# An expert layer's routing in 16 bits, its list and table steps interleaved on VectorE, and a reordered opening of the next layer

## The chip, the cores and the metric

The kernel runs on one core of one Trainium2 chip. The metric is the device time of one execution in microseconds (us). TensorE is called PE here, VectorE DVE, ScalarE ACT, GpSimd POOL; SyncE (SP) issues most of the DMA transfers.

## What is computed

The input x has 4 batches of 512 rows with 288 channels; a condition vector per batch gives shifts, scales and gates. Three transformer layers follow one another, each with 16-head attention. The first one's feed-forward part is a mixture of experts (2 of 4, 1152 hidden channels each), the two others have one dense part. The last stage rotates the rows in the plane of 64 orthonormal columns.

```python
def _L0_cond_ref(x, c, w_adaln, b_adaln, w_qkv, b_qkv, w_proj, b_proj, w_gate, w1, b1, w2, b2):
    ...
    x = x + g_msa[:, None, :] * o
    xn = _modulate(_ln(x), sh_mlp, sc_mlp)
    xf = xn.reshape(-1, C)
    gate_logits = xf @ w_gate
    topk_logits, topk_idx = jax.lax.top_k(gate_logits, TOP_K)
    gates = jax.nn.softmax(topk_logits, axis=-1)
    ...
    hmid = jax.nn.gelu(jnp.einsum('tc,ech->eth', xf, w1) + b1[:, None, :], approximate=True)
    eo = jnp.einsum('eth,ehc->etc', hmid, w2) + b2[:, None, :]
    moe = jnp.einsum('te,etc->tc', cw, eo).reshape(B, N, C)
    return x + g_mlp[:, None, :] * moe
...
U, _ = jnp.linalg.qr(P)
R = _rotation(cond, W, b)
z = jnp.einsum('btn,nd->btd', x, U)
z_rot = jnp.einsum('btd,bde->bte', z, R)
x_rot = x + jnp.einsum('btd,nd->btn', z_rot - z, U)
```

## The kernel before

**Orders.** No scheduler is at work. The order of the instructions on each engine is written out by hand, and semaphores stand between the engines. Each engine takes its queue strictly in order, so a wait on one instruction holds all that stand behind it. A product in 32 bits is made of three passes over operands split into a high and a low part: ACT rounds the high part, DVE subtracts to get the low part, and PE multiplies high by high, high by low and low by high. DVE's dependent small steps are joined by `link` (a semaphore that DVE raises and then waits for itself).

**Routing in layer one.** For each batch b, DVE computes from the gate logits which two of the four experts a row chooses (`gate_ranks(b)`, the tile `rank` of zeros and ones, and `rank_totals`). PE multiplies `rank` by a strictly triangular matrix and by ones (`ranks(b)`, L2033 to L2039), which gives every row its number within its expert; `slots(b)` on DVE turns them into slot numbers, `slot_hits(b)` compares these with a ramp, and `tokens(b)` on PE (L2073, L2077) finds the rows of the first tile with them. `keep_clock(bank, n)` on PE issues n dummy products (L2045).

**Tiles.** The 2048 rows, each chosen twice, are gathered in 11 tiles of up to 512 rows of one expert. A unit j is (tile t, chunk m) = divmod(j, 9): the hidden chunk `tile_hidden(j)` (L1636, 7 matmuls of 512 columns), gelu and high part on ACT, the low part `tile_parts(j)` on DVE (L2992), and two units later `tile_second(j - 2)` on PE (L2114, 12 matmuls of 288 columns). Which rows go in which tile is known late: `first_tokens` casts the list of tile 0 (L2802), POOL gathers its rows with four indirect transfers, and PE turns them (`turn_first`, L2064), with ACT and DVE making high and low part (`first_low`, L2970 and L2973). `tile_places` and `tile_table` (L2878 to L2937) are some 45 small DVE steps that work out the place and the expert of every tile. For the lists of tiles 1 to 10, `list_hits(b)` (L2825 eight times, L2827 once) makes one-hot rows and columns of batch b, `list_products(b)` on PE (L2052) multiplies them, and `token_lists` casts the sum (L2832). SP waits for that cast, loads each list as an index (L769), and POOL gathers the rows of tile 1. `turn_tile(1, c)` (L2089) turns them, one chunk c of three after each of units 6, 7 and 8.

**Weights.** `split_lo_first(0, kind, i)` are low parts of tile 0's weights (kind "1" for the first product, "2" for the second, three pieces each: L3130 with the tail L3131, and L3127); the later tiles' pieces are split at fixed units (`tile_pieces`). SP's loads stand in a fixed order: a big weight of the last stage (L828) after the landing of tile 1's rows, and tile 2's weights behind it.

**Afterwards.** `gate_weights` computes the two mixing weights of each row and `row_places` the place of each row's two results in the stored output (L2939 to L2950). In layer two's opening, POOL gathers the results by them, ACT weighs them (`weigh(k, b)`, L1433), DVE adds them to the residual (`combine_pair(b)`), normalises batch b (`moments`, `rsqrt`, `normalise`, ends in L2498), PE turns the normalised rows (L1699) at the places that `TURN_AT[1]` names, ACT modulates them (`turned`, L1423 and L1427), DVE makes the low part (`low`), and PE multiplies by the weights of queries, keys and values. In `TURN_AT`, the key (b, m) means: after the m-th product of batch b (0 to 4 queries and keys, 5 to 8 values); the value (b', chunks) names what is turned there. A finished chunk leaves PE's bank by ACT (`qk_hi`) and DVE (`qk_rest`, L2535).

## Time and profile before

| | us |
|---|---|
| median of three runs (1562.21 to 1564.72) | 1562.62 |
| the profiled execution | 1557.15 |
| its span | 1555.4 |
| PE busy in it | 1444.6 (93%) |
| DVE busy | 1220.6 (78%) |
| ACT busy | 931.0 (60%) |
| POOL busy | 724.0 (47%) |

The span is the time from the first to the last recorded instruction of the profiled execution; the time around it is 1.75 us. Busy shares are means over the whole span, and PE leads over most of it: what counts for the time is where PE stands still. A row of a timeline gives start, length, engine, line, operation, what is written and read, the shape, the count of records, and in brackets the idle time before it with what ended it. The length of one row may overlap the next, so steps are best read from start to start.

### The profile page before, as it was taken

To read this page: it belongs to the slowest core of one execution; us is meant where nothing else is said; L and a number is where in the kernel's file an instruction comes from. 1 tells how busy PE (TensorE), PEld (TensorE's weight loads), DVE (VectorE), ACT (ScalarE), POOL (GpSimd) and SP (SyncE) were. 2 spreads that over 40 slices of the span, in tenths; PEclk is the share of its full clock that TensorE was granted. 3 is DMA by queue.
4 is the path that set the end of the run, shared out by engine and by line. 5 is a ranking of instruction groups with operands and counts; after the bars stand their busy time and mean duration, and the time that the engine had idled before them with its cause. 6 is when DMAs were issued, how large, how long until landed. Compare 5 with 4: busy or idle time off the path is not lost.

```text
span 1555.4 us, 26822 instructions
## 1 busy us (share of the span) xinstructions
PE 1444.6 (93%) x8987; PEld 986.7 (63%) x8987; DVE 1220.6 (78%) x2469; ACT 931.0 (60%) x1687; POOL 724.0 (47%) x1620
## 2 busy tenths in 40 slices
PE   6899999996999999996999998888999999899998
PEld 5653334875999988885633345877865333378885
DVE  7789996886898687668889987677967999866643
ACT  4458887543666654565478886434734888754432
POOL 0555650114566533036556667676766666650000
PEclk9999999988999999997999999999998999999999
DMA  7765530127555654336735423101165453100001
GB/s 209 227 172 125 144 82 2 38 86 228 160 154 131 184 136 125 93 121 200 237 84 153 115 38 47 6 5 21 18 204 164 119 141 91 6 3 1 1 1 61
DMA packets 108245, 160.70 MB, mean 103 GB/s; under 512 B 33860, under 2 KB 75830, under 8 KB 107976
## 3 DMA queue, kind: packets, MB, share of 16 engines
q1 hardware_dynamic: 101964, 142.85, 30.2%
q0 software_dynamic: 6144, 16.14, 8.5%
q8 instruction: 72, 1.18, 0.3%
q14 instruction: 65, 0.53, 0.1%
HBM read 114.74 MB, written 39.58 MB: 99 GB/s over the span
## 4 chain that ended last, share of the span: by engine, by line
PE 72%; DVE 18%; issue 3%; ACT 3%; DMA 2%; POOL 1%; SPq 1%; DVEq 0%; ACTq 0%; POOLq 0%
PE psum L1636 22%; PE psum L1826 12%; PE psum L1815 9%; PE psum L1789 9%; PE psum L2114 7%; PE psum L2252 5%; DVE bn L2462 1%; PE psum L1699 1%; PE psum L1965 1%; DVE hid_lo L3146 1%; POOL moe_y_end L1179 1%; DVE x_norm L2490 1%; PE psum L2392 1%; PE psum L2089 1%; DVE minus_max L2650 1%
## 5 line engine op out<-in xcount | busy, mean ns | idle before, releaser
L1555 ACT ACTIVATE probs<-psum 128x512 f32<-128x512 f32 x768 | 401.9, 601 | 85.9 <-PE psum L1815 85.3
L2650 DVE TENSOR_REDUCE minus_max<-psum 128x1 fp32r<-128x512 f32 x450 | 288.3, 682 | 36.5 <-PE psum L1789 35.1
L1636 PE MATMUL psum<-x_split,w_hi 128*128 128x512 f32 (+1 forms) x684 | 246.4, 403 | 17.0 <-issue 6.1
L1789 PE MATMUL psum<-k_stack,q_stack 54*128 54x512 f32 x768 | 245.5, 455 | 11.6 <-DMA k_stack<-qk_parts_d 3.3
L1815 PE MATMUL psum<-q_stack,k_stack 55*128 55x512 f32 x768 | 243.2, 450 | 0.6 <-ACT probs L1555 0.6
L1082 POOL TENSOR_TENSOR qr_m<-qr_m 64x8 f32<-64x8 f32 (+35 forms) x544 | 198.4, 365 | 42.6
L1826 PE MATMUL psum<-probs,o_t 128*19 128x512 f32 x1536 | 206.4, 610 | 6.1 <-ACT o_t L1534 3.2
L2645 DVE TENSOR_REDUCE minus_max<-psum 128x2 fp32r<-128x1024 f32 x159 | 193.7, 1218 | 19.8 <-PE psum L1789 19.6
L1789 PEld LDWEIGHTS psum<-k_stack,q_stack 54*128 54x128 f32 x768 | 116.1, 188 | 132.4 <-DVE minus_max L2650 60.6
L1815 PEld LDWEIGHTS psum<-q_stack,k_stack 55*128 55x128 f32 x768 | 118.9, 188 | 127.0 <-ACT probs L1555 116.1
L1077 POOL TENSOR_TENSOR qr_m<-qr_rows 64x288 f32<-64x288 f32 (+31 forms) x64 | 45.5, 711 | 247.9 <-DMA qr_rows<-qr_rows 247.9
L1636 PEld LDWEIGHTS psum<-x_split,w_hi 128*128 128x128 f32 x684 | 130.8, 193 | 41.6 <-issue 10.6
L1636 PE MATMUL psum<-x_split,w_lo 128*128 128x512 f32 (+1 forms) x342 | 133.5, 390 | 0.0
L1589 ACT ACTIVATE hid_f<-psum 128x512 f32<-128x512 f32 x72 | 42.9, 596 | 135.6 <-PE psum L1636 134.0
L1391 ACT ACTIVATE hid_f<-psum 128x512 f32<-128x512 f32 (+1 forms) x99 | 55.4, 559 | 109.1 <-PE psum L1636 104.1
L2114 PE MATMUL psum<-w_hi,hid_hi 128*128 128x288 f32 x360 | 107.9, 300 | 3.2 <-DVE hid_lo L2992 3.0
L2992 DVE TENSOR_TENSOR hid_lo<-hid_f,hid_hi 128x512 fp32r<-128x512 f32 (+1 forms) x99 | 67.2, 679 | 54.4 <-ACT hid_hi L1341 53.0
L1167 POOL DMA_INDIRECT tile_rows<-moe_rows_d,tile_tokens x40 | 48.3, 1206 | 128.8 <-DMA tile_tokens<-token_lists 85.2
L2114 PE MATMUL psum<-w_hi,hid_lo 128*128 128x288 f32 x360 | 107.3, 298 | 0.0
L2114 PE MATMUL psum<-w_lo,hid_hi 128*128 128x288 f32 x360 | 107.3, 298 | 0.0
L1636 PE MATMUL psum<-x_split,wqkv_hi 128*128 128x512 f32 (+1 forms) x240 | 92.4, 426 | 7.5 <-DVE qk_parts L2535 5.8
L3146 DVE TENSOR_TENSOR hid_lo<-hid_f,hid_hi 128x512 fp32r<-128x512 f32 x72 | 51.8, 720 | 53.0 <-ACT hid_hi L1356 52.4
(431 smaller groups left out, 3246.6 us busy)
## 6 DMA issues: line engine op xcount, KB each, us to landing
qk_parts_d<-qk_parts SPq DMA_DIRECT2D x48, 512.0 KB, 4.6
raw_b<-in_L_cond_w SPq DMA_DIRECT2D x36, 432.0 KB, 4.0
q_stack<-qk_parts_d SPq DMA_DIRECT2D x96, 144.0 KB
k_stack<-qk_parts_d SPq DMA_DIRECT2D x96, 144.0 KB
raw_a<-in_L_cond_w SPq DMA_DIRECT2D x36, 384.0 KB
q_stack<-qk_parts_d SPq DMA_DIRECT2D x96, 72.0 KB
k_stack<-qk_parts_d SPq DMA_DIRECT2D x96, 72.0 KB
moe_out_d<-branch SPq DMA_DIRECT2D x9, 576.0 KB, 3.3
```

The lines of the kernel that those rows point to most:

```text
L1082: step(gp.tensor_tensor(QM1[:, :, 0:h], QM1[:, :, 0:h], QM1[:, :, n - h:n], ALU.add))
L1555: act.activation(PE_[:, v // 4, 2 * hf + pr, :], psum[:, score_bank(16 * i + v), :], ACT.Exp, scale=SCALE).then_inc(s_e, 1)
L1636: i = pe.matmul(dst, a, r, start=(n == 0), stop=(n == len(terms) - 1))
L1789: return pe.matmul(psum[:, bank, :], Q6[half(hf, STK), g, pr, P * qt:P * qt + P], K6[half(hf, STK), g, pr, :], start=True, stop=True)
L1815: pe.matmul(psum[:, score_bank(n), :], K6[rows, g, pr, P * kt:P * kt + P], Q6[rows, g, pr, :], start=True, stop=True).then_inc(s_st, 1)
L1826: mm = pe.matmul(psum[32 * h:32 * h + VW, 6, :], values_of(b, kt)[:, g, h, 0:VW], PE_[:, kt, h, :], start=(kt == 0), stop=(kt == TT - 1))
L2114: mm = pe.matmul(psum[:, 4 + q, 0:C], h[:, m % 3, c], w[:, m, :], start=(m == 0 and n == 0), stop=(m == HM - 1 and n == 2))
L2252: mm = pe.matmul(psum[:, 4 + t, 0:C], h[:, m % 3, c], w[:, m, :], start=(m == 0 and n == 0), stop=(m == HM - 1 and n == 2))
L2645: dve.tensor_reduce(MX[:, i % 2, u:u + 9:8], psum[:, bank:bank + 2, :], AX.X, ALU.max, negate=True).then_inc(s_mx, 1)
L2650: dve.tensor_reduce(MX[:, i % 2, col:col + 1], psum[:, bank, :], AX.X, ALU.max, negate=True).then_inc(s_mx, 1)
L2992: dve.tensor_tensor(HL[:, m % 3, 0:w], HF[:, j % 2, 0:w], HH[:, m % 3, 0:w].bitcast(F32), ALU.subtract).then_inc(m_h, 1)
L3146: dve.tensor_tensor(HL[:, m % 3, :], HF[:, i % 2, :], HH[:, m % 3, :].bitcast(F32), ALU.subtract).then_inc(s_h, 1)
```

## The change

- `rank`, `rank_totals` and the two constant matrices become bfloat16, and `keep_clock(0, 1)` ahead of `ranks(3)` is gone.
- `slots(2)` and `gate_ranks(3)` are interleaved in one function, `last_ranks`: a step of the one stands where the other waits.
- The nine instructions of `list_hits(0)` stand one by one in link gaps of `tile_places`, those of `list_hits(1)` in gaps of `tile_table` (`link_over`); hits 2 and 3 follow at units 1 and 2. The list products move ahead by one or two units, the first ahead of unit 0.
- The pieces of tile 0's weight splits go in another order.
- Tile 1 is turned after units 7 (two chunks, one in another bank) and in unit 8, not after 6, 7 and 8.
- `gate_weights` moves from unit 5 to 9, `row_places` from 7 to 12, with storage of their own.
- In layer two's opening batch 1's turned chunks are modulated ahead of the weighing of batch 2, and the turns in `TURN_AT[1]` move.

```diff
+FIRST_PIECES = (("1", 0), ("1", 1), ("2", 0), ("1", 2), ("2", 1), ("2", 2))
...
-           {(0, 6): (1, (0, 1)), (0, 7): (1, (2,)), (0, 8): (2, (0, 1)), (1, 3): (2, (2,)), (1, 6): (3, (0,)), (1, 7): (3, (1,)),
-            (2, 0): (3, (2,))},
+           {(0, 4): (1, (0, 1)), (0, 6): (1, (2,)), (1, 1): (2, (0,)), (1, 2): (2, (1,)), (1, 5): (2, (2,)), (1, 8): (3, (0, 1, 2))},
...
-        RK = new("rank", [P, NT, EXPERTS], F32)
+        RK = new("rank", [P, NT, EXPERTS], BF16)
+        RTS = new("rank_totals", [P, B + 1, EXPERTS], BF16)
...
+            if t == 0:
+                return {HM - 2: (0, 1), HM - 1: (2,)}.get(m, ())
...
                 weigh(1, 1)
-                qk_hi(1, 0, (0,))
+                qk_hi(1, 0, (0, 1))
                 split_hi_qkv(1, 2)
-                qk_hi(1, 0, range(1, QN))
+                qk_hi(1, 0, (2, 3, 4))
                 split_hi("p", 1, RAWP, WPH, WPT, s_rb, RB["p", 1])
+                turned(1, 0, 1, (0,))
                 values(1, 0, (0,))
+                turned(1, 0, 1, (1,))
+                values(1, 0, (1,))
+                turned(1, 0, 1, (2,))
                 weigh(0, 2)
-                turned(1, 0, 1, (0,))
-                values(1, 0, (1,))
+                values(1, 0, (2,))
                 weigh(1, 2)
-                turned(1, 0, 1, (1, 2))
...
-                keep_clock(0, 1)
                 ranks(3)
...
                 turn_first()
+                list_products(0)
                 for j in range(MOE_UNITS + 2):
                     t, m = divmod(j, HM)
                     if j < MOE_UNITS:
                         tile_hidden(j)
+                    if j == 4:
+                        list_products(3)
+                    if j == HM - 1:
+                        turn_tile(1, 2)
                     if j >= 2:
                         tile_second(j - 2)
...
+            def link_over(i, b, n):
+
+                i.then_inc(s_dv, 1)
+                steps[0] += 1
+                list_hit(b, n)
+                dve.wait_ge(s_dv, steps[0])
...
                 slot_hits(1)
-                slots(2)
-                gate_ranks(3)
+                last_ranks()
...
                 split_lo_first(0, "1", 0)
-                split_lo_first(0, "2", 0)
+                tile_places()
+                for c in range(KC + 1):
+                    first_low(0, c)
                 split_lo_first(0, "1", 1)
-                tile_places()
-                for h in range(2):
-                    for c in range(KC + 1):
-                        first_low(h, c)
+                for c in range(KC + 1):
+                    first_low(1, c)
                 tile_table()
...
-                    if j < B:
-                        list_hits(j)
+                    for c in turned_at(t, m):
+                        tile_low(t + 1, c)
+                    if j == 0:
+                        split_lo_first(0, "2", 0)
+                    if j == 1:
+                        list_hits(2)
+                    if j == 2:
+                        list_hits(3)
                     if j == 3:
-                        split_lo_first(0, "2", 1)
                         split_lo_first(0, "1", 2)
                         token_lists()
                     if j == 4:
+                        split_lo_first(0, "2", 1)
                         split_lo_first(0, "2", 2)
-                    if j == 5:
+                    if j == HM:
                         gate_weights()
-                    if j == 7:
+                    if j == HM + 3:
                         row_places()
```

On DVE, behind the cast of the first tokens, this stood before: the weight splits, then the start of `tile_places`.

```order
L3130 TENSOR_TENSOR w_lo<-raw_a,w_hi 128x2x256
L3131 TENSOR_TENSOR w_tail<-raw_a,w_tail 33x256
L3127 TENSOR_TENSOR w_lo<-raw_b,w_hi 128x864
L3130 TENSOR_TENSOR w_lo<-raw_a,w_hi 128x2x384
L3131 TENSOR_TENSOR w_tail<-raw_a,w_tail 33x384
L2885 TENSOR_TENSOR is_tile<-psum,ramp_188 128x16
L2886 TENSOR_TENSOR is_whole<-psum,ramp_188 128x4
L2887 TENSOR_SCALAR key_limits<-ramp_188 128x16
L2888 TENSOR_TENSOR tile_value<-ramp_188 128x16
L2890 COPY tile_place_in_order<-ramp_188 128x9
```

This stands there now, with the first hits (`list_rows`) between the steps of the places:

```order
L2965 TENSOR_TENSOR is_tile<-psum,ramp_189 128x16
L2966 TENSOR_TENSOR is_whole<-psum,ramp_189 128x4
L2967 TENSOR_SCALAR key_limits<-ramp_189 128x16
L2968 TENSOR_TENSOR tile_value<-ramp_189 128x16
L2970 COPY tile_place_in_order<-ramp_189 128x9
L2972 MEMSET tile_place_in_order 128x1 x2
L2973 SCALAR_TENSOR_TENSOR is_whole<-psum,ramp_189 128x12
L2844 TENSOR_SCALAR list_rows_104<-list_places,slot_rows,token_scale 128x128
L2975 MEMSET is_tile 128x1
L2976 MEMSET is_whole 128x1
L2844 TENSOR_SCALAR list_rows_104<-list_places,slot_rows,token_scale 128x128
L2977 SCALAR_TENSOR_TENSOR chunk_keys<-is_whole,ramp_189 128x16
```

One split of kind "2" and one of kind "1" no longer stand ahead of `tile_places`, and one hit stands in each of its link gaps.

On PE, this stood around the turn of tile 1's second chunk, behind unit 7's hidden chunk and before unit 8's (`tile_rows` are the gathered rows):

```order
L2114 MATMUL psum<-w_hi,hid_lo 128x288
L2089 MATMUL psum<-ident,tile_rows_118 128x128 x4
L1636 MATMUL psum<-x_split,w_hi 128x512
L1636 MATMUL psum<-x_split,w_lo 128x512
L1636 MATMUL psum<-x_split,w_hi 128x512 x2
L1636 MATMUL psum<-x_split,w_lo 128x512
L1636 MATMUL psum<-x_split,w_hi 128x512
L1636 MATMUL psum<-x_tail,w_tail 128x512
L2114 MATMUL psum<-w_hi,hid_hi 128x288
```

Now the first two chunks are turned together, and the third between the hidden chunk of unit 8 and the second product of unit 6:

```order
L2125 MATMUL psum<-w_hi,hid_lo 128x288
L2100 MATMUL psum<-ident,tile_rows_118 128x128 x8
L1644 MATMUL psum<-x_split,w_hi 128x512
L1644 MATMUL psum<-x_split,w_lo 128x512
L1644 MATMUL psum<-x_split,w_hi 128x512 x2
L1644 MATMUL psum<-x_split,w_lo 128x512
L1644 MATMUL psum<-x_split,w_hi 128x512
L1644 MATMUL psum<-x_tail,w_tail 128x512
L2100 MATMUL psum<-ident,tile_rows_118 96x128 x4
L2125 MATMUL psum<-w_hi,hid_hi 128x288
```

The turn that stood after unit 6 is gone to the place of the second, so a hidden chunk and a second product more lie before the first of them.

On DVE in layer two's opening, this stood from the normalising of batch 2 (`x_norm_88`) to the combination of batch 3 (`moe_y_end_122`):

```order
L2490 TENSOR_SCALAR x_norm_88<-residual,ln_stats,rstd 128x288 x4
L2498 COPY x_norm_88<-x_norm_88 128x4x32 x2
L2506 TENSOR_TENSOR x_split<-x_mod_89,x_split 128x1024
L2508 TENSOR_TENSOR x_tail<-x_mod_89,x_tail 32x512
L3022 TENSOR_TENSOR moe_y_end_122<-moe_y_end_122,branch 128x1152
L3024 TENSOR_TENSOR moe_y_end_122<-moe_y_end_122,gate_mlp 128x1152
L3026 TENSOR_TENSOR residual<-residual,moe_y_end_122 128x1152
L2535 TENSOR_TENSOR qk_parts<-psum,qk_parts 128x512
```

Now the low part of batch 1 (`x_split`, `x_tail`) stands ahead of the combination of batch 2 (`moe_y_end_120`):

```order
L2551 TENSOR_TENSOR qk_parts<-psum,qk_parts 64x512
L2522 TENSOR_TENSOR x_split<-x_mod_89,x_split 128x1024
L2524 TENSOR_TENSOR x_tail<-x_mod_89,x_tail 32x512
L3102 TENSOR_TENSOR moe_y_end_120<-moe_y_end_120,moe_y_end_121 128x1152
L3104 TENSOR_TENSOR moe_y_end_120<-moe_y_end_120,gate_mlp 128x1152
L3106 TENSOR_TENSOR residual<-residual,moe_y_end_120 128x1152
L2478 BN_STATS bn_160<-residual 128x6 x4
```

The low part of batch 1 has moved past the whole combination and normalising of batch 2.

## Rows read from the trace of the kernel before

**Rows 1.** Timeline of PE (start, length, instruction, idle time before and its end), tile 0.
```profile
335.84 0.47 PE L1636 MATMUL psum<-x_split,w_hi 128*128 128x512 f32 x1 [1.90 <-DVE x_tail L2973]
...
353.94 0.50 PE L1636 MATMUL psum<-x_split,w_hi 128*128 128x512 f32 x1 [2.40 <-DVE w_tail L3131]
...
367.87 1.11 PE L2089 MATMUL psum<-ident,tile_rows 128*128 128x128 f32 x4 [5.69 <-DMA tile_rows<-moe_rows_d,tile_tokens]
...
371.69 0.30 PE L2114 MATMUL psum<-w_hi,hid_hi 128*128 128x288 f32 x1
...
381.47 0.47 PE L1636 MATMUL psum<-x_split,w_hi 128*128 128x512 f32 x1 [3.92 <-issue]
```

**Rows 2.** Windows: busy time of PE, PEld, DVE, ACT, POOL; clock, DMA share, GB/s.
```profile
318.00:326.00 8.00, 7.99 (x55) 6.61 (x54) 5.28 (x26) 5.63 (x9) 0.09 (x1) 0.50 0.24 87
354.00:358.00 4.00, 4.00 (x13) 3.45 (x14) 3.47 (x7) 1.04 (x2) 0.93 (x1) 0.57 0.03 3
358.00:362.00 4.00, 4.00 (x27) 3.64 (x25) 3.50 (x11) 2.24 (x4) 3.08 (x4) 1.00 0.77 235
362.00:366.00 4.00, 0.18 (x2) 0.00 (x0) 0.76 (x2) 0.00 (x0) 3.09 (x4) 0.84 1.00 310
382.00:386.00 4.00, 4.00 (x16) 3.42 (x16) 1.22 (x3) 1.23 (x2) 3.26 (x11) 0.60 0.97 304
```

**Rows 3.** Timeline of PE, last ranks and dummy products.
```profile
318.89 1.42 PE L2035 MATMUL psum<-rank,all_ones 128*128 128x12 f32 x6
...
321.45 2.91 PE L2045 MATMUL psum<-slot_numbers,ident 128*128 128x256 f32 x6
```

**Rows 4.** Timeline of DVE, last slots and token column.
```profile
321.20 0.18 DVE L2868 TENSOR_TENSOR slots<-psum,ramp 128x16 f32<-128x16 f32 x1 [1.64 <-PE psum L2039]
...
324.87 0.16 DVE L2802 CAST tile_tokens<-psum 128x4 uint32<-128x4 f32 x1 [0.80 <-PE psum L2077]
```

**Rows 5.** Timeline of DVE, a weight split and the second table's start.
```profile
326.13 1.06 DVE L3127 TENSOR_TENSOR w_lo<-raw_b,w_hi 128x864 fp32r<-128x864 f32 x1
...
335.73 0.17 DVE L2921 SCALAR_TENSOR_TENSOR tile_place<-chunks_ahead 128x16 f32<-128x16 f32 x1
335.82 0.17 DVE L2922 TENSOR_SCALAR half_place<-chunks_ahead 128x16 f32<-128x16 f32 x1
336.02 0.17 DVE L2923 TENSOR_TENSOR tile_place<-tile_place,half_place 128x16 f32<-128x16 f32 x1
```

**Rows 6.** Timeline of DVE, last list hits and token lists.
```profile
348.61 1.87 DVE L2825 TENSOR_SCALAR list_rows<-list_places,slot_rows,token_scale 128x128 f16<-128x128 f16 x8
350.40 0.69 DVE L2827 TENSOR_TENSOR list_columns<-list_places,slot_columns 128x512 f16<-128x512 f16 x1
...
353.92 0.22 DVE L2832 CAST token_lists<-psum 128x64 uint32<-128x64 f32 x1
```

**Rows 7.** Timelines of DVE and ACT, row places, last low part, tile 2's weights.
```profile
375.15 0.17 DVE L2943 TENSOR_TENSOR place_offsets<-tile_place,ramp 128x16 f32<-128x16 f32 x1
...
380.68 0.68 DVE L2985 TENSOR_TENSOR x_tail<-psum,x_tail 32x512 fp32r<-32x512 f32 x1
...
394.09 0.84 ACT L1267 ACTIVATE w_hi<-raw_a 128x768 fp32r<-128x768 f32 x1
```

**Rows 8.** Timeline of PE, layer two's opening.
```profile
719.65 1.97 PE L1699 MATMUL psum<-ident,x_norm 128*128 128x128 f32 x8 [10.76 <-DVE x_norm L2498]
...
740.21 0.40 PE L1636 MATMUL psum<-x_split,wqkv_hi 128*128 128x512 f32 x1
```

**Rows 9.** Timelines of ACT and DVE, layer two's opening.
```profile
709.20 0.76 ACT L1423 ACTIVATE x_mod<-psum,mod_cols 128x512 f32<-128x512 f32 x1
709.99 0.63 ACT L1427 ACTIVATE x_split<-x_mod 128x512 fp32r<-128x512 f32 x1
...
709.33 1.36 DVE L3022 TENSOR_TENSOR moe_y_end<-moe_y_end,moe_y_end 128x1152 f32<-128x1152 f32 x1 [3.05 <-ACT moe_y_end L1433]
...
724.45 1.36 DVE L3022 TENSOR_TENSOR moe_y_end<-moe_y_end,branch 128x1152 f32<-128x1152 f32 x1 [3.03 <-ACT branch L1433]
```

227 lines of the change are left out of this document (141 added, 86 removed).

## The prediction

> **What bounds the kernel now.** I read three views, in this order: the waits of TensorE (PE), to find where it stands still; the timelines of the engines around each gap, to find what is late; the windows, for the granted clock and the load of the DMA engines. From 335.84 to 381.47 us, in the first tile of the expert layer, PE shows four gaps in its row of products: 1.90 before unit 0, 2.40 before unit 5, 5.69 before the turn of tile 1 and 3.92 before tile 1 itself [rows 1]; each row's bracket is the idle time ahead of it and what ended it. They come to 13.9 us. Each is due to a full VectorE (DVE) queue, the third by way of a list cast late and a gather, the fourth (given as issue, with no releaser in the trace) as DVE's timeline shows below. After each longer one the clock is lower for some us: 0.57 of full speed in 354 to 358 us against 1.00 in the next four, 13 matmuls against 27; 0.60 in 382 to 386 [rows 2]. In layer two's opening PE stands still once for 10.76 us, for the normalised rows of batch 2 [rows 8]. Everything the change touches lies in these two places, and between them I find nothing that it moves.
>
> **Ranks and tokens.** PE does the last ranks at half clock (0.50 in 318 to 326 us [rows 2]): the six products against all_ones alone take 1.42 us, two records for each of three instructions [rows 3]. DVE takes them up for its last slots after waiting 1.64 us, until 321.20, and gets the last token column at 324.87 [rows 4]. In 16 bits I expect one record for two; the floor of the cost is nothing and the ceiling half of today's, so the wait of 1.64 us goes in either case. DVE's two chains interleaved save about 1.0: a linked step follows its forerunner at 0.20 us, an unlinked one at 0.09 [rows 5], and some ten of the links now have work of the other chain in them. Ranks reach PE at about 317.4, slots(3) run right behind DVE's slot hits at 318.5, and then the three dummy products (2.91 us at half clock [rows 3]) bind: the last token column at 322.0, which is 2.9 earlier. Bounds: 2.5 (nothing from the interleaving) to 4 (dummies at full clock).
>
> **Tables and first units.** From the token column to the start of the second table DVE takes 335.73 - 324.87 = 10.86 us [rows 4, 5]. Taken out: one split of layer-one weights, 1.06 [rows 5]. Put in: nine list hits in the link gaps. A list row costs 0.224 (1.79 for eight) and the columns 0.60 [rows 6]; a link gap hides 0.20 - 0.09 = 0.11 of each, so eight rows and the columns come to 8 x 0.11 + 0.5 = 1.4 net. So 10.86 - 1.0 + 1.4 = 11.3, the second table starts at 333.3 and unit 0 at 333.4 (before 335.84): -2.4. The bound below is full hiding (0.5), the bound above none at all (2.4 for each table).
>
> Here one rule speaks against the edit. The Trainium skill ("VectorE: DVE Perf Modes", section "The DRAIN you can't avoid") says that DVE's pipe empties after each operation, that a semaphore between operations costs nothing extra, and that one should minimise the count of operations and not of semaphores. By that a hit in a gap would cost its full time, 2.4 for each table in place of 1.4, and the gain below would be about 2 smaller. The spacing of 0.09 against 0.20 [rows 5] does not bear it out for operations this small, so I go by the row.
>
> The second table lasts 3.3 + 1.4, to 338.0; the first low half of a hidden chunk comes at 338.7 and the moved split behind it at 339.7. PE has three hidden chunks done at 338.2, so a new wait of about 1.5 stands before the second product of unit 0. From there DVE has 3.1 us per unit (0.69 + 2.4) for hits 2 and 3 (a low half 0.69 and the 2.4), level with PE: a unit's 19 matmuls at 27 in 4 us [rows 2] are 2.8, and about 0.4 of list products. Unit 5 starts at 348.6 and the gap of 2.40 before it goes. Unit 5 waits for the tail of the weight split, which now ends at 348.5 and not 353.9: DVE has no hits at j=3 (2.39 [rows 6]) and one split less (1.0) there, and starts 2.0 sooner. The token lists are cast right behind it, at 348.5, against 353.92 [rows 6]. **Term 1: the gathered rows of tile 1 land 5.4 earlier, at 362.5.** Their path (cast, load of the index, gather, landing) is untouched and took 13.95 us, from 353.92 to 367.87.
>
> **The turn of tile 1.** Today 381.47 - 367.87 = 13.60 us pass from landed rows to tile 1's first product [rows 1]: three turns, each behind a unit, and a wait of 3.92 for the last low part. DVE did row_places from 375.15 and the last tail only at 380.68 [rows 7]. After: PE does unit 7 and second 5 ahead of the turns, arrives at 358.5 and waits 4.0 for the rows; then two turns (about 1.8), hidden 8 at low clock (turn and hidden chunk behind today's wait take 371.69 - 367.87 = 3.8 [rows 1], some 3.0 without the turn), the third turn (0.5) and second 6 (1.6) under which ScalarE and DVE make the last high and low part. That is 7.0 with the low part done, with row_places out of the way: tile 1 starts at about 369.4. **Term 2: 6.9 for 13.6, -6.7.** Should PE come later than I reckon, this holds until the wait of 4.0 is used up.
> **Term 3:** no gap stands before tile 1, so the stretch at 0.60 (4 x 0.40 = 1.6 lost) goes, less 0.2 of remainder: **-1.4**.
> **Term 4:** from 362 us the DMA engines are full (1.00, then 0.97 in 382 to 386 [rows 2]) with a large weight of the last stage ahead of tile 2's weights. What they carry starts 5.4 earlier and PE 13.5 earlier, so tile 2's first piece, split on ScalarE at 394.09 [rows 7] with no wait, would be wanted at 380.6 and land at some 382 to 383. ScalarE holds the next gelu behind it: 2 us on ScalarE, of which PE's double buffer takes half. **+1.0**, from 0 to 5.
> gate_weights (now at unit 9) and row_places (at unit 12) are about 5 us of DVE. They move to where DVE waits for ScalarE for more than 2 us per unit, and nobody needs them before the combination: nothing. Without that cover they would delay a low part by at most 2.8.
>
> **Layer two's opening.** DVE starts batch 2's combination at 709.33 and batch 3's at 724.45, each after a wait for ScalarE's weighing [rows 9]. Now batch 1's three turned chunks (0.76 and 0.63 each, 4.2 in all [rows 9]) stand ahead of batch 2's weighing on ScalarE, so the combination starts at about 713.4, and the norm that ended PE's gap at 719.65 comes at 723.7. But batch 1's low part (1.9) is already made, so PE does two chunks of batch 1's queries and keys in between, some 3.4 us that it does today behind the gap, and the waits for its banks there get fewer. Batch 3 is bound by its gather and starts when it does now. Batch 2's first chunk, today at 740.21 [rows 8], comes at 739.1. **Term 5: -1.2**, from -3 to +3.5.
>
> **The sum.** -5.4 - 6.7 - 1.4 + 1.0 - 1.2 = -13.7. The profiled execution took 1557.15 us (span 1555.4), so it would take 1543.4. The median shown is 5.5 above it; on that scale 1562.62 - 13.7 = **1548.9**. 0.2% (3.1 us) is about what a measurement of this kernel can tell from no change.
>
> **Rivals.**
> *The weights of tile 2 bind (0.13).* The DMA engines are full from 362 us on and get only 5.4 us, so PE would give back all that it gained beyond that: -5.4 - 1.4 - 1.2, or 1554.6. For it: 1.00 and 0.97 in the windows. Against: the piece at 394.09 was not waited for and had slack.
> *The opening turns against itself (0.12).* PE needs the norm of batch 2 before it has anything else; it comes 4.1 late, and only part is covered: +3.5 in place of -1.2, or 1553.6. For it: the wait is the longest of all. Against: the two chunks that are brought forward.
> *The hits are not hidden (0.07).* A row costs its full 0.224 and the columns 0.60, 1.0 more in each table; unit 0 and the lists come later by up to 2, which gives 1551. By the rule of the Trainium skill named above ("VectorE: DVE Perf Modes") this would be the likeliest case; the 0.09 in [rows 5] speaks against it.
> *Slower (0.04).* The clock. A dummy product is gone and the ranks have half the records, so PE does less before unit 0. At half clock a unit costs about 3.0 more (19 matmuls at 4/13 and at 4/27 us [rows 2]). Should the clock stay low through tile 0 this passes the gain from 4.6 units on; all nine give +13, or 1576. Against it: today the clock rose by itself after the dummies, nine of which stay.
> *No change to be seen (0.04).* The first two together with the third (-8.0 + 4.7 + 1 = -2.3), or 1560.3; or 16-bit ranks and places that DVE makes no sooner.
> The forecast has 0.60.
>
> **Range and chances.** The forecast's own bounds (term 4 to 5, term 5 from -3, token column to -4) give 1545 to 1553. To hold 8 in 10 it must take in the first rivals as well: 1544.5 to 1556.5. Faster by over 0.2%: 0.60 + 0.13 + 0.12 + 0.07 = 0.92; within: 0.04; slower: 0.04.
>
> **What would show it.** In the profile after: no wait for all_ones products on DVE and the token column near 322.0; unit 0 near 333.4; a new wait of some 1.5 before unit 0's second product; the token lists near 348.5 with rows near 362.5 and a wait of about 4 there; tile 1 at 369 with no gap; in the opening a gap of about 8 us that ends near 724 less the 12 gained. Wrong would be: a wait of ScalarE on weights after tile 1's third unit that lasts over 3 us, a clock below 1 for whole units of tile 0, or an opening whose first chunk of batch 2 comes less than 12 us earlier than 740.21.

## The result, and the profile after

The changed kernel took 1558.74 us in the median of 20 runs (1550.54 to 1569.18), the kernel before 1562.63 in as many, run in turns with it. The ratio of the two is 0.9958, with a 95% interval of 0.9939 to 0.9977: 6.6 us less, between 3.6 and 9.5. The forecast was 13.7 less. Its sign was right, and it promised about twice what came.

The profiled execution of the changed kernel took 1563.31 us, which is 6 more than that of before. This is the first thing to read rightly, so first the page of after (span, then part 1: busy us, share of the span, instructions):

```profile
span 1561.6 us, 26773 instructions
...
PE 1439.9 (92%) x8963; PEld 979.6 (63%) x8963; DVE 1217.8 (78%) x2469; ACT 931.0 (60%) x1687; POOL 720.1 (46%) x1620
```

PE's timeline in tile 0 (the columns are those of [rows 1]):

```profile
335.84 0.47 PE L1644 MATMUL psum<-x_split,w_hi 128*128 128x512 f32 x1 [2.18 <-DVE x_tail L3053]
...
351.39 0.40 PE L1644 MATMUL psum<-x_split,w_hi 128*128 128x512 f32 x1
...
364.58 1.97 PE L2100 MATMUL psum<-ident,tile_rows 128*128 128x128 f32 x8 [3.42 <-DMA tile_rows<-moe_rows_d,tile_tokens]
...
371.52 0.47 PE L1644 MATMUL psum<-x_split,w_hi 128*128 128x512 f32 x1 [0.88 <-issue]
...
391.12 0.97 PE L2100 MATMUL psum<-ident,tile_rows 128*96 128x128 f32 x4 [2.05 <-DVE x_split L3062]
```

Against [rows 1]: unit 5 (351.39) starts with no gap, the rows of tile 1 land 3.29 earlier (364.58) and tile 1 starts 9.95 earlier (371.52). This execution, however, came to the expert layer 2.36 us later: DVE's last copy of the logits is at 316.13, against 313.77 before. Counted from that copy these steps gain 2.36 more, and unit 0, which starts at 335.84 in both, is 2.36 earlier too. That copy stands between 313.19 and 318.47 in the twenty traces at hand, so all that follows is counted from it. The last row is new: PE waits 2.05 in tile 1, at a turn of tile 2's rows.

DVE's timeline, token column, the beginning of the second table and its end, the last split and the token lists:

```profile
324.76 0.16 DVE L2820 CAST tile_tokens<-psum 128x4 uint32<-128x4 f32 x1 [1.14 <-PE psum L2085]
...
335.72 0.18 DVE L3001 SCALAR_TENSOR_TENSOR tile_place<-chunks_ahead 128x16 f32<-128x16 f32 x1
335.82 0.17 DVE L3002 TENSOR_SCALAR half_place<-chunks_ahead 128x16 f32<-128x16 f32 x1
335.89 0.31 DVE L2844 TENSOR_SCALAR list_rows<-list_places,slot_rows,token_scale 128x128 f16<-128x128 f16 x1
336.12 0.17 DVE L3003 TENSOR_TENSOR tile_place<-tile_place,half_place 128x16 f32<-128x16 f32 x1
...
340.18 0.69 DVE L3072 TENSOR_TENSOR hid_lo<-hid_f,hid_hi 128x512 fp32r<-128x512 f32 x1
...
350.77 0.22 DVE L2864 CAST token_lists<-psum 128x64 uint32<-128x64 f32 x1
```

A hit (0.31 long) stands between two linked steps, and the second of these, L3003, starts 0.30 after L3002 instead of 0.20 [rows 5]: a hit costs a tenth of a us there. PE did its first units at a low clock in this execution (0.79 in 336 to 344, against 1.00 before), which the prediction named as a sign of being wrong. It cost nothing: PE then had no wait before unit 0's second product, where e0, at 1.00, has one of 1.06, and unit 5 starts as far behind the copy in both (35.26 and 34.92).

Windows of after (busy us of PE, PEld, DVE, ACT, POOL; clock, DMA share, GB/s), and ACT's timeline at tile 2's first piece:

```profile
362.00:366.00 4.00, 1.42 (x7) 1.43 (x8) 1.22 (x2) 0.44 (x2) 3.32 (x4) 0.75 1.01 283
366.00:370.00 4.00, 4.00 (x23) 3.52 (x22) 2.44 (x3) 3.00 (x6) 0.49 (x1) 0.83 1.04 323
380.00:384.00 4.00, 4.00 (x28) 3.70 (x27) 2.81 (x7) 1.67 (x3) 2.80 (x4) 1.00 0.97 309
384.00:388.00 4.00, 3.86 (x26) 3.32 (x25) 1.96 (x3) 2.01 (x4) 3.27 (x10) 1.00 1.05 314
388.00:392.00 4.00, 1.95 (x14) 1.70 (x13) 3.82 (x11) 1.97 (x4) 3.53 (x9) 0.91 1.06 338
392.00:396.00 4.00, 4.00 (x18) 3.38 (x18) 3.76 (x11) 2.32 (x4) 1.65 (x2) 0.66 0.62 198
```

```profile
385.89 0.85 ACT L1276 ACTIVATE w_hi<-raw_a 128x768 fp32r<-128x768 f32 x1 [3.40 <-DMA raw_a<-in_L_cond_b]
```

DMA is full and ACT waits 3.40 for the piece. Gelu and turns stand behind it. PE stands still in 388 to 392 and then does 18 matmuls in 4 us at a clock of 0.66, against 28 at 1.00. The slow stretch of [rows 2], which lay at the start of tile 1, has gone from there (the first unit of tile 1 lasts 3.28 for 4.83 before) and has come up again four units later, where the fifth and sixth unit last 6.12 and 4.64 for 3.68 and 3.29.

Layer two's opening: PE's two long waits, then DVE's combinations of batches 2 and 3, then ACT:

```profile
700.72 1.54 PE L1707 MATMUL psum<-ident,x_norm 128*128 128x128 f32 x6 [4.23 <-DVE x_norm L2514]
...
715.47 0.62 PE L1644 MATMUL psum<-wqkv_hi,x_split 128*128 128x304 f32 x1 [6.90 <-ACT o_t L1537]
...
731.94 1.12 PE L1707 MATMUL psum<-ident,x_norm 128*128 128x128 f32 x4 [10.28 <-DVE x_norm L2514]
```

```profile
720.49 1.51 DVE L3102 TENSOR_TENSOR moe_y_end<-moe_y_end,moe_y_end 128x1152 f32<-128x1152 f32 x1 [3.04 <-ACT moe_y_end L1437]
...
732.41 1.35 DVE L3102 TENSOR_TENSOR moe_y_end<-moe_y_end,branch 128x1152 f32<-128x1152 f32 x1
```

```profile
531.18 0.93 ACT L1284 ACTIVATE w_hi<-raw_b 128x864 fp32r<-128x864 f32 x1 [7.30 <-remote]
...
714.99 0.42 ACT L1537 ACTIVATE o_t<-psum 128x304 f32<-128x304 f32 x1 [6.38 <-remote]
```

Where [rows 8] show one wait of 10.76 there are three. A wait of 2.40 for a bank, at 699.20 before, is down to 0.70. The one of 6.90 hangs on ACT, which stood for 6.38 us on something that no engine, queue or transfer in the trace released ("remote"). The same happened in tile 5, for 7.30 us, and near the end of the tiles, for 3.05. The trace of before has no such stall, so the two profiles can't be subtracted as they stand.

The spans in sections, each from a start to a start: L is DVE's last copy of the logits, landed is PE's first turn of tile 1, the opening reaches from the first product of the last expert unit to the same product of layer two's first attention in every kernel (the seventh pair of `k_stack` and `q_stack`, 755.46 before), and each of the other sections starts with the first product of its first unit. Runs e0 to e17 are told below.

| us | before | after | e2 | e0 |
|---|---|---|---|---|
| L to unit 0 | 22.07 | 19.71 | 21.64 | 19.67 |
| L to landed | 54.10 | 48.45 | 54.64 | 48.15 |
| landed to tile 1 | 13.60 | 6.94 | 13.23 | 7.10 |
| tile 1 | 32.09 | 34.51 | 30.34 | 31.48 |
| tile 2 to tile 6 | 151.39 | 155.22 | 151.40 | 152.56 |
| tile 7 to last unit | 118.03 | 118.57 | 118.03 | 118.70 |
| opening | 72.49 | 84.19 | 76.00 | 76.22 |
| from there to the end | 799.95 | 797.57 | 793.18 | 792.65 |

### The profile page after: what moved, and what is told of

Same layout as the page of the kernel before. It is cut to its first block, busy times and chain, and to the rows that moved or that the text cites. A ratio compares the mean times of both kernels' runs of the same rounds, so it can differ in the third digit from the quotient of the medians.

```text
span 1561.6 us, 26773 instructions
## 1 busy us (share of the span) xinstructions
PE 1439.9 (92%) x8963; PEld 979.6 (63%) x8963; DVE 1217.8 (78%) x2469; ACT 931.0 (60%) x1687; POOL 720.1 (46%) x1620
## 4 chain that ended last, share of the span: by engine, by line
PE 55%; DVE 16%; ACT 3%; issue 3%; DMA 2%; another core or an unknown queue 1%; SPq 1%; POOL 0%; DVEq 0%; ACTq 0%
PE psum L1644 18%; PE psum L1834 8%; PE psum L1823 6%; PE psum L2125 6%; PE psum L1797 6%; PE psum L2268 5%; DVE bn L2478 1%; PE psum L1707 1%; DVE x_norm L2506 1%; DMA raw_a<-in_L_cond_b 1%; DVE hid_lo L3229 1%; PE psum L1973 1%; PE psum L2408 1%; PE psum L2100 1%
## 5 line engine op out<-in xcount | busy, mean ns | idle before, releaser
L1091 POOL TENSOR_TENSOR qr_m<-qr_m 64x8 f32<-64x8 f32 (+35 forms) x544 | 194.9, 358 | 42.6
L3229 DVE TENSOR_TENSOR hid_lo<-hid_f,hid_hi 128x512 fp32r<-128x512 f32 x72 | 51.9, 721 | 51.8 <-ACT hid_hi L1362 51.2
```

Source lines behind the costliest of these rows:

```text
L1091: step(gp.tensor_tensor(QM1[:, :, 0:h], QM1[:, :, 0:h], QM1[:, :, n - h:n], ALU.add))
L3229: dve.tensor_tensor(HL[:, m % 3, :], HF[:, i % 2, :], HH[:, m % 3, :].bitcast(F32), ALU.subtract).then_inc(s_h, 1)
```

## The experiments

Each ratio is against the kernel before on the same chip. Five chips were used: A (e0 to e3), B (e4 to e7), C (e8 to e11), D (e12 to e15), E (e16, e17).

**e0_after_again**: the changed kernel as it is.

> The changed kernel once more, unaltered. Theory A (the new opening costs time by its order): layer two's opening is again some 5 to 12 us longer than before, and its norm of batch 2 comes late. Theory B (the 6.4 us in which ScalarE stood still in the opening with nothing that the trace names are an accident of that one execution): that stall is absent and the opening is level with before within 2 us. Either way: tile 1 starts 12 us nearer to the last logit rows, tile 2's first weights are waited for by about 3.4 us on ScalarE, and the time is 0.4 to 0.8% under before.

Measured: 1540.98 against 1554.68, ratio 0.9918 [0.9897, 0.9938], so -12.7 us, with a span of 1542.6 in the profile. ACT has no stall here. Up to tile 1 the sections are those of after within 0.3. Tile 1, where ACT waits 1.99 for the piece of weights instead of 3.40, is 3.0 shorter, tiles 2 to 6 are 2.7 shorter and the opening 8.0. The last two hold ACT's stalls in after, so the stalls belong to an execution and not to the kernel. The opening is still 3.7 longer than before, which is more than theory B and less than theory A had it.

**e2_opening_only**: the kernel before, with the new opening alone.

```diff
@@ TURN_AT[1], and opening_1 of ACT and DVE
-{(0, 6): (1, (0, 1)), (0, 7): (1, (2,)), (0, 8): (2, (0, 1)), ...}
+{(0, 4): (1, (0, 1)), (0, 6): (1, (2,)), (1, 1): (2, (0,)), ...}
```

> The kernel before with the new opening alone. Theory A: slower than before by 3 to 8 us. Theory B and my forecast of -1.2: within 2 us of before.

**e1_old_opening**: the reverse, the changed kernel with the opening of before.

> The change with the opening of layer two as it was before. Theory A: faster than the changed kernel by 4 us or more, about 1551, which is 11 below before. Theory B: within 2 us of the changed kernel.

Measured: e2 0.9998 [0.998, 1.0017], opening 76.00; e1 0.9912 [0.988, 0.9943], opening 72.20. In the profile the new opening is 3.5 (e2 against before) to 4.0 (e0 against e1) longer, where 1.2 less was forecast. In the timed rounds of this chip nothing of it is seen: -0.3 us for e2 (its interval reaches from -3.1 to +2.6), and e0 and e1 differ by 0.9. DVE's combinations, first of e0 (last unit at 673.69), then of e1 (670.97):

```profile
705.25 1.36 DVE L3102 TENSOR_TENSOR moe_y_end<-moe_y_end,moe_y_end 128x1152 f32<-128x1152 f32 x1 [3.04 <-ACT moe_y_end L1437]
...
717.63 1.34 DVE L3102 TENSOR_TENSOR moe_y_end<-moe_y_end,branch 128x1152 f32<-128x1152 f32 x1
```

```profile
698.21 1.36 DVE L3097 TENSOR_TENSOR moe_y_end<-moe_y_end,moe_y_end 128x1152 f32<-128x1152 f32 x1 [3.94 <-ACT moe_y_end L1438]
...
712.16 1.36 DVE L3097 TENSOR_TENSOR moe_y_end<-moe_y_end,branch 128x1152 f32<-128x1152 f32 x1 [1.86 <-ACT branch L1438]
```

Counted from the last unit, batch 2's combination comes at 31.6 in place of 27.2, and batch 3's at 43.9 in place of 41.2. In e0 the latter has no bracket: DVE takes it up straight after batch 2's norm and one chunk. ACT's weighing of the second operand, first of before (last unit at 682.97) and then of e0, shows that this had been ready:

```profile
722.60 1.82 ACT L1433 ACTIVATE branch<-branch,logits 128x288 f32<-128x288 f32 x4 [1.95 <-DMA branch<-moe_out_d,row_places]
```

```profile
712.36 1.81 ACT L1437 ACTIVATE branch<-branch,logits 128x288 f32<-128x288 f32 x4 [2.10 <-DMA branch<-moe_out_d,row_places]
```

In both it follows the gather's landing, 39.6 and 38.7 after the last unit. So the gather is no later. In before the combination followed at once, after DVE had waited 3.03 for it; in e0 it starts 3.5 after the weighing's end, held by DVE's queue, and that by batch 2.

**e5_weigh_early**: ACT weighs batch 2 ahead of batch 1's first turned chunk.

```diff
@@ opening_1 of ACT
+                weigh(0, 2)
                 turned(1, 0, 1, (0,))
...
                 turned(1, 0, 1, (2,))
-                weigh(0, 2)
```

> The changed kernel with the weighing of batch 2's first half ahead of batch 1's turned chunks on ScalarE, which stands idle there for 3.8 us. If VectorE's late start of batch 2's combination is what costs time in the opening: it starts 2 us sooner (at 29.5 for 31.5 us after the last unit's start), batch 3's combination and the end of the opening too, so that the stretch up to batch 2's attention goes from 75 or 76 to 73 or 74. Rival (something else, such as PE's wait of 4.2 for the norm of batch 1): the stretch stays within 0.7.

Measured: 1538.97 against 1552.75, 0.9932 [0.9903, 0.9961]; opening 73.60, the shortest with the new order (e4, e6 and e7, with the changed kernel's opening, have 75.5, 75.5 and 76.2 on this chip):

```profile
697.68 1.36 DVE L3102 TENSOR_TENSOR moe_y_end<-moe_y_end,moe_y_end 128x1152 f32<-128x1152 f32 x1 [1.33 <-ACT moe_y_end L1437]
...
709.06 1.36 DVE L3102 TENSOR_TENSOR moe_y_end<-moe_y_end,branch 128x1152 f32<-128x1152 f32 x1 [0.52 <-ACT branch L1437]
```

From the last unit (668.23) these are 29.5 and 40.8: with batch 2's combination 2.1 earlier than in e0, batch 3's comes 3.1 earlier, and now it does wait. So in e0 batch 3 was held by batch 2; here its own gather and weighing bind it again, by 0.52. The whole doesn't tell e5 from e4 and e6 (0.9936 each).

**e3_weights_first**: SyncE issues the first piece of tile 2's weights ahead of the last stage's large weight, and DVE uses that large weight one unit later.

```diff
@@ the unit at which DVE uses the large weight
-SKEW_UNIT, EXPM_UNIT = 10, 66
+SKEW_UNIT, EXPM_UNIT = 11, 66
@@ SyncE, before the last stage's large weight
+                e = tile_expert(2)
+                load_tile_w1(2, 0, e)
+                load_tile_w2(2, 0, e)
...
-                        load_tile_w1(t + 2, 0, e)
-                        load_tile_w2(t + 2, 0, e)
+                        if t >= 1:
+                            load_tile_w1(t + 2, 0, e)
+                            load_tile_w2(t + 2, 0, e)
```

> The changed kernel with the first weights of tile 2 loaded ahead of the last stage's big weight, whose use moves one unit later. If the order of the loads is what costs time in tile 1: ScalarE's wait of 3.4 us goes, no gap in tile 1's fourth to sixth unit, tile 2 starts 3 to 4 us sooner, total -3. Rival (the DMA engines as such are the bound): the wait moves to VectorE's use of the big weight or to the next piece, and less than 1 us is won.

Measured: 0.9921 [0.9898, 0.9945]. ACT takes the piece up with no wait, and tile 1 lasts 30.33, as in e2, against 31.48 in e0 and 34.51 in after. So in tile 1 the piece costs e0 1.15 and after 4.2. What it costs differs by execution: with the loads in the changed kernel's order ACT waits for it between not at all (e5, e7) and 3.40 (after), and tile 1 lasts 30.4 to 34.5. Tiles 2 to 6 last 151.38 in e3 and 152.56 in e0. That difference lies in one unit of tile 2, where PE waits 0.98 for DVE; whether the piece is behind it is not shown, since e9, which has e3's edit, is 0.9 long there too. The -3 that was expected of the whole didn't come: e3 and e0 have the same ratio.

**e7_turns_back**: tile 1's turns behind units 6, 7 and 8, as before.

```diff
@@ turned_at
-                return {HM - 2: (0, 1), HM - 1: (2,)}.get(m, ())
+                return (m - 6,) if 6 <= m <= 6 + KC else ()
```

> The changed kernel with tile 1 turned after units 6, 7 and 8 as before. If the new places of the turns carry the 6.7 us: from landed rows to tile 1's first product about 10 us (13.6 less the row places' 2.8 and the low part's wait), 3 more than in the changed kernel, total +3. Rival (the row places alone carry it): within 1 us of 7.0.

**e6_places_back**: `gate_weights` and `row_places` at units 5 and 7 again (`if j == 5`, `if j == 7` for `HM` and `HM + 3`).

> The changed kernel with the gate weights at unit 5 and the row places at unit 7 again. The prediction puts the gap ahead of tile 1 down to the row places: then the way from landed rows to tile 1's first product grows from 7.0 to about 9.8 us if they run behind the landing, but they may run in the wait for the rows; theory C is that they do, since unit 7 now stands ahead of that wait: no change there (under 0.5).

**e4_one_dummy**: one dummy product in place of three (`keep_clock(0, 1)`).

> The changed kernel with one dummy product in place of three ahead of the last token column. If the dummies bind, as the prediction said: the token column comes 1.5 to 1.9 us nearer to the last logit rows (7.0 for 8.6), and unit 0 starts about 1.5 sooner. Rival (VectorE's last slot hits bind): the column moves by less than 0.6. Second rival (the clock): the column comes sooner but PE runs units 0 to 2 at half clock for longer, and unit 5 starts no sooner.

Measured: e7 0.996 [0.994, 0.998], e6 0.9936 [0.9908, 0.9963], e4 0.9936 [0.9914, 0.9958]. From landed to tile 1, e7 takes 11.99, e6 8.23, e4 7.05 and e5 7.85. The turns' order is 4 to 5 of the 6.7 us that this section lost, and the whole of e7 gives back about 4. For the places nothing is shown: 8.23 is hardly above the 6.8 to 8.1 that kernels without this edit take, and from L to tile 1 e6 (56.94) is level with e5 (56.88). In e7 PE waits longer for the rows, since it has fewer products to do ahead of the first turn, and then once more in front of tile 1:

```profile
363.43 1.11 PE L2097 MATMUL psum<-ident,tile_rows 128*128 128x128 f32 x4 [8.72 <-DMA tile_rows<-moe_rows_d,tile_tokens]
...
375.42 0.47 PE L1644 MATMUL psum<-x_split,w_hi 128*128 128x512 f32 x1 [1.45 <-issue]
```

In e4 the token column comes 7.75 after L and not 8.60, and unit 0 gains 0.45: two dummies (1.9 us of PE) had held the column up by 0.85, half of the 1.5 to 1.9 expected.

**e10_f32_ranks**: ranks, their totals and the two constant matrices in 32 bits again, all else as changed.

> The changed kernel with ranks, totals and constant matrices in 32 bits again. If the ranks' second record and VectorE's wait for them matter as the prediction has it: VectorE waits again 1.3 to 1.7 us for its last slots, the token column comes 0.7 to 1.7 later than 8.6, and unit 0 by as much. Rival (the three dummies cover it): the column within 0.3.

**e11_hits_in_blocks**: the interleaved chains stay, but the nine hits stand in a block behind each table.

```diff
@@ link_over
-                i.then_inc(s_dv, 1)
-                steps[0] += 1
-                list_hit(b, n)
-                dve.wait_ge(s_dv, steps[0])
+                link(i)
```

> The changed kernel with the first two batches' list hits in a block behind each table and not in its link gaps. By the spacing of linked and unlinked steps each gap hides 0.11 of a hit: unit 0 comes 0.9 to 1.0 later for the first block, the lists 1.8 to 2.0 later for both. By the rule that the pipe empties after every operation and a semaphore costs nothing: no difference at either place (under 0.3).

**e8_after_third**: the changed kernel again, beside them. **e9_all_three**: it with the edits of e3, e4 and e5.

> The changed kernel a third time, unaltered. The first comparison gave -0.42%, the second -0.82%. If the two differ because ScalarE stood still in some executions for reasons outside the program: about -0.8% again, no unexplained stall in the profile, and the segments of the second profile within 1 us each. If the smaller figure is the true one: between -0.3 and -0.6%.

> The changed kernel with the early weighing, tile 2's first weights ahead of the big weight, and one dummy product in place of three. The three gains are in different stages, so they add: 2 to 3 in the opening, 1 in tile 1, 0.5 ahead of unit 0: 3 to 4 us under the changed kernel, some 15 under before. Rival: they collide (the gather of tile 1's rows lands when it did), and only the opening's 2 show.

Measured: e8 0.9944 [0.9922, 0.9966], e9 0.9958 [0.9932, 0.9984], e10 0.9964 [0.9941, 0.9988], e11 0.998 [0.9961, 0.9998]. In e10 the token column comes 8.75 after L, for 8.60 to 8.64 in the others with three dummies, which is 0.15 later. This is the price of 32-bit ranks at full clock. The kernel before did its last ranks at half clock [rows 3], and in after the clock falls just where the 16-bit ranks run (319.72); in e10 it had not yet fallen. The stretch around the last ranks, in after and in e10:

```profile
320.00:322.00 2.00, 1.14 (x20) 1.02 (x19) 1.83 (x12) 2.00 (x3) 0.00 (x0) 0.50 0.81 301
```

```profile
320.00:322.00 2.00, 1.98 (x44) 1.89 (x43) 1.86 (x10) 2.00 (x5) 0.00 (x0) 1.00 0.28 104
```

The six products against `all_ones`, in e10 and then in e14 (told below), whose routing is that of the kernel before, and e14's token column:

```profile
321.19 0.81 PE L2043 MATMUL psum<-rank,all_ones 128*128 128x12 f32 x6
```

```profile
320.77 0.81 PE L2038 MATMUL psum<-rank,all_ones 128*128 128x12 f32 x6
```

```profile
325.21 0.16 DVE L2807 CAST tile_tokens<-psum 128x4 uint32<-128x4 f32 x1 [0.27 <-PE psum L2080]
```

They take 0.81 there and 1.42 before. With them at full clock the old routing has its column 9.37 after L (315.84) in e14, against 11.10 in before, 11.09 in e12 and 10.68 in e2. The 2.5 that the column gained from before to after (11.10 to 8.63) are made up, in DVE's timelines, of 1.1 for the interleaved chains (from the start of `slots(2)` to the hits of batch 2 3.40 before and 2.31 now), 1.7 for the last ranks (2.77 and 1.05 from these hits to the last slots), and -0.3 for the dummies behind them. Of the 1.7 e10 keeps 1.2. So 16 bits are worth 0.15 where the clock is full, and by an estimate from these rows up to 1.4 where it is not; no run shows 32-bit ranks at half clock in the changed kernel. The dummy ahead of the last ranks, which the change took out, had held nothing up: in e2, e12 and e14 PE waits 0.55 more behind it for DVE's totals. Whether it bears on the clock is not shown.

In e11 unit 0 starts 20.74 after L (after: 19.71) and unit 5 37.14 (35.26). The end of its second table, with the block and the first low half behind it:

```profile
336.41 0.17 DVE L2998 SCALAR_TENSOR_TENSOR tile_place<-chunks_ahead 128x16 f32<-128x16 f32 x1
...
339.55 0.16 DVE L3014 CAST tile_table<-tile_expert 128x11 int32<-128x11 f32 x1
339.62 1.88 DVE L2844 TENSOR_SCALAR list_rows<-list_places,slot_rows,token_scale 128x128 f16<-128x128 f16 x8
341.40 0.70 DVE L2847 TENSOR_TENSOR list_columns<-list_places,slot_columns 128x512 f16<-128x512 f16 x1
342.00 0.69 DVE L3069 TENSOR_TENSOR hid_lo<-hid_f,hid_hi 128x512 fp32r<-128x512 f32 x1
```

Table and hits take 5.59 (336.41 to 342.00) in blocks and 4.46 (335.72 to 340.18) interleaved. The gaps hide 1.1 of 2.4 per table. The token lists come 2.2 later than in e8 (36.34 and 34.14 after L), as expected. From there to the landing the rows took 16.0 in e11 and 14.0 in e8, which the hits don't explain, and tile 1 starts 4.4 later (59.46 and 55.01). The whole points the same way: e11 gains 3.1 us and e8 8.8. e10, with 5.6, is not told apart from e8.

e8 gains 8.8 us (0.56%, between the result's 0.42% and e0's 0.82%) and has stalls of ACT in its profile. e9 does not beat e8 on this chip, where 3 to 4 were expected: its opening is 83.73 and e8's 84.88, with ACT stalls in both. In tile 1 it shows the rival that was named for e3. ACT takes up tile 2's piece with no wait, but DVE then waits for the large weight, which now comes behind it:

```profile
388.31 0.46 DVE L3273 SCALAR_TENSOR_TENSOR l_junk<-l_w,silu_c_all 126x288 f32<-126x288 f32 x1 [2.70 <-DMA skew_bias<-in_L_cond_b]
```

PE waits 1.51 for the turn behind it, and tile 1 lasts 32.05, not 30.33.

**e12 to e15** ask for the stalls and the opening on one more chip: the kernel before (e12), e1 again (e13), e2 again (e14), and the changed kernel with its one small gelu ahead of tile 0 cut into twelve (e15), which shifts each later instruction of ACT by eleven places.

```diff
@@ ACT, e15
-                act.activation(SCT[:, 0, :], SCT[:, 1, :], ACT.Gelu_apprx_tanh)
+                for k in range(12):
+                    act.activation(SCT[:, 0, k:k + 1], SCT[:, 1, k:k + 1], ACT.Gelu_apprx_tanh)
```

> The kernel before, unaltered, with a profile from the same chip as the three others. If ScalarE's unexplained stalls are a property of the chip alone: they are here too in tile 5, and in the opening they fall into ScalarE's wait for the gather (6.6 us), so that the opening stays near 72. If they come with the change: none.

> The change with the old opening. Where ScalarE stalls, the old opening hides it behind the gather and the new one does not: the opening is 72 here against 84, and the time 6 to 12 us under the changed kernel's on such a chip (about -1.0% against before). On a chip without stalls the opening is 3 us shorter and the time is within 3 us. Rival: the stall moves along and the opening is as long.

> The kernel before with the new opening. On a chip with stalls: opening 84, slower than before by 6 to 12 us. On a chip without: 75, and +0 to +3.

> The changed kernel with eleven more tiny instructions on ScalarE before the first tile, in idle time. If the stalls belong to places in ScalarE's instruction stream: they hit instructions eleven places earlier in the program. If they belong to what the instructions wait for: the same instructions stall. On a chip without stalls: nothing is told, and the time is that of the changed kernel within 1 us.

Measured: e12 1.0006 [0.9986, 1.0027], e13 0.9951 [0.9927, 0.9974], e14 1.0027 [1.0004, 1.0051], e15 0.9964 [0.9945, 0.9982]. The kernel before stalls too, and its opening is 83.02, so it doesn't hide the stall, as was expected of it. From ACT's timeline of e12, and below it of the trace of before at the same instruction:

```profile
730.68 0.78 ACT L1423 ACTIVATE x_mod<-psum,mod_cols 128x512 f32<-128x512 f32 x1 [12.28 <-remote]
731.49 0.63 ACT L1427 ACTIVATE x_split<-x_mod 128x512 fp32r<-128x512 f32 x1
```

```profile
705.85 0.77 ACT L1423 ACTIVATE x_mod<-psum,mod_cols 128x512 f32<-128x512 f32 x1
706.65 0.63 ACT L1427 ACTIVATE x_split<-x_mod 128x512 fp32r<-128x512 f32 x1
```

In e15 the stalls in tile 5 (3.33 and 5.13), in tile 8 (2.50) and in the opening (9.56) are at the splits, hidden chunks and copies at which e14, e16 and e8 stall (instructions 805, 807, 950 and 1095 of ACT), though each stands eleven places later in ACT's stream; so they go with what happens then and not with a place in that stream. The openings are 83.02 (e12), 83.92 (e13), 83.98 (e14) and 84.74 (e15). These are 8 to 12 us more than on chips A and B, and the orders are only 1 apart (e14 against e12, e15 against e13), where 12 were expected.

**e16_old_opening_weights** and **e17_weigh_early_weights**: the changed kernel with the edit of e3 and the opening of before (e16) or of e5 (e17).

> The changed kernel with the opening of before and with tile 2's first piece of weights issued ahead of the waited-for ones: both steps that went against the forecast are taken back. If they are all that is missing on a chip without ScalarE's stalls, the profile shows the opening at 72 us from the last unit's start and tile 1 at about 30.3, and the ratio is 0.991 (-14) there; on a chip with the stalls the opening is 82 to 83 and the ratio 0.993 to 0.995. Rival: the opening of before is worth nothing in the whole, since its later batches give the time back; then the ratio is that of e17 within 0.1%.

> The changed kernel with batch 2's weighing on ScalarE ahead of batch 1's first turned chunk, and with tile 2's first piece of weights issued first; the new opening stays otherwise. By the theory that the opening is held by batch 2's and 3's combinations on DVE, it lasts 73 us, 1 more than with the opening of before, and the kernel is 1 us slower than e16. Rival: the two are equal, since nothing that the opening gains or loses by a us or two reaches the end.

Measured: e16 1554.41 against 1566.67, 0.9925 [0.99, 0.995], -11.8 us; e17 0.9942 [0.9914, 0.9969], -9.1. The openings are 82.65 and 83.65, and tile 1 lasts 30.33 in both. e16 is the fastest of the kernels tried on a chip with stalls, e5 had the lowest time of all; neither is told apart from its neighbours by its interval.

## Why the prediction was wrong

**Term 1** (-5.4): right in size, in part for another reason. Rows landed 5.65 earlier after L (after against before) and 6.5 earlier on one chip (e0 against e2). Single executions spread widely here: 52.5 to 55.6 with the old routing, 47.9 to 51.2 with the new one (without e11). Of its steps the token column gained 2.5 (forecast 2.9), unit 0 2.4 and 2.0 (2.4), the table with hits grew by 1.25, from 3.21 to 4.46 (1.4), and the new wait before unit 0's second product is 1.1 in e0 (1.5) and not there in after. The rival of unhidden hits fell with e11. There the rule of the Trainium skill ("VectorE: DVE Perf Modes", section "The DRAIN you can't avoid") does not hold for operations this small, as the prediction read it: by that, e11 would have equalled e8, and its unit 0 comes 1.05 later. The same section adds that a next operation that is not held starts earlier, and the 0.09 of [rows 5] agree with that. The reason given for 16-bit ranks, that one record in two goes, is not borne out at full clock (0.15 in e10) and is untested at half clock. The interleaved chains gave their 1.1 (forecast 1.0). The forecast also said that slot hits and dummies bind once the ranks are fast, and e4 that the dummies do by 0.85.

**Term 2** (-6.7): right in size, and in the main part of its cause. 6.94 for a forecast 6.9; e7 gives back 4 to 5 of it, and that row_places had to go is not shown (e6).

**Term 3** (-1.4): right between these two traces. Tile 1's first unit lasts 3.28 for 4.83, which is -1.55. With the old routing it is 3.28 in e2 as well, and 6.00 in e14, so this stretch too differs by execution.

**Term 4** (+1.0, from 0 to 5): right in mechanism, its size left to chance. By tile 1 against e3 it is +4.2 in after, +1.15 in e0 and nothing in e5 and e7. I had priced the wait on tile 2's piece alone, as half of 2 us on ACT. It was 3.40 in after and 1.99 in e0, and in after it stopped PE at a turn (2.05) behind which the clock fell to 0.66. With term 3 tile 1 should have lost 0.4; it grew by 2.4 in after and lost 0.6 in e0. The 5 us of gate_weights and row_places, put at nothing, now stand in tile 1, where DVE is 3.8 of 4 us busy (388 to 396 in after); that they cost nothing there is not shown, but e6, which takes them back, is no faster than e4 and e5.

**Term 5** (-1.2): the step that failed is "Batch 3 is bound by its gather and starts when it does now". The first half was so: ACT's weighing waited for the gather, 1.95 in before and 2.10 in e0. The second half did not follow. The combination stands behind batch 2's combination and norm in DVE's queue and had 3.03 us to spare [rows 9]. Batch 2 came 4.3 (e0 against e1) to 5.7 (e2 against before) later (forecast 4.1), the 3.03 were used up, and batch 3 came 2.8 later; e5 moved both back together. A second step was missing: batch 1's turn, put ahead, meets a norm that isn't there yet, and PE waits 4.2 for it; the shorter wait for a bank (2.40 to 0.70) gives back 1.7 of this. By the profiles the term is +3.5 to +4.0, which is the rival "the opening turns against itself" (+3.5), to which I gave 0.12.

**The sum again**, by what the profiles show: -12.3 (after against before) and -12.6 (e0 against e2) for terms 1 and 2; +2.4 and +1.1 for terms 3 and 4 (tile 1 alone), and in e0 1.2 more in tile 2; +3.5 to +4.0 for the opening. Together this is -5.9 to -8.0, and the result is -6.6. That the two agree is partly luck, since the timed rounds weigh the opening otherwise on chip A, as told next. Both small terms gone wrong, with everything else as forecast, was no case of its own: I had put them together only with hits that aren't hidden, at 0.04, and each alone otherwise.

**What stays open.** The timed rounds don't weigh the opening alike on all chips, so that it costs 3.5 to 4.0 is shown for the profiles' section and not for the whole. On chip A it costs nothing (e2 -0.3, e1 0.9 below e0), on D +4.2 (e14) and +2.0 (e15 against e13), on E +2.7 (e17 against e16, where e5's edit takes part of it back). The changed kernel as it is gains 12.7 on A, 8.8 on C and, as e15, 5.6 on D; e4, e5 and e6, which are near it, gain 9.9 to 10.6 on B. A and B (before: 1553 to 1555) are the chips whose profiles have no stall of ACT, and C, D and E (1565 to 1567) those whose profiles have some. The chip of the result itself lies between them (1562.6), with no stall in the profile of before and three in that of after. That the change is worth less where ACT stalls agrees with all of this, but no run shows how the two act on each other, and what ACT waits for there isn't in the trace. Nor is it shown where on chip A the 3 to 4 us of the opening come back: the part after it differs by up to 10 us between single executions of near kernels.

## What to carry to other kernels

A wait with a named releaser says what came last, and its length is what the engine has to spare there. Before calling a unit of work independent of what is moved ahead of it, look at how long its wait is and what stands before it in its own queue; a delay larger than the wait passes through. Before pricing a narrower type by one run, look at the clock at which each kernel ran the instructions concerned. When an edit brings a whole engine forward, list what it will ask for next at the earlier time and price the miss with its followers, the clock among them. And give small terms that can fail together a case of their own, because their sum may be half of the gain.

## What the runs showed of the hardware

- ACT stalls of 2 to 12 us that nothing in the trace releases, at a few places of tiles 5, 6 and 8, the end of the tiles and the opening, in both kernels, in the executions on chips C, D and E and in that of after, and in none of those read on chips A and B. The program is 10 to 14 us slower on such chips (before: 1565 to 1567 against 1553 to 1555).
- DVE: the second of two linked operations of 128x16 starts 0.20 after the first. A list hit put between them, which takes 0.22 in a row of its like, costs 0.10 there (336.12 against 335.82), so a little over half of it is hidden.
- TensorE's granted clock can differ between executions at the same instructions. The kernel before did its last 32-bit ranks at 0.50 (1.42 us for six products against `all_ones`, token column 11.10 after L), and the same routing did them at 1.00 in e14 (0.81, and 9.37).
- Two dummy products less (e4, 2 us of PE at half clock) left the clock at 1.00 in 336 to 344. With all three it was 1.00 in e0 and 0.79 in after, so the dummies don't decide it.
